# Attention of a graph network kernel: x into the output projection's banks at the start, bias rows by TensorE, softmax over heads by reduces

## The reference

```python
q = (x @ Wq + bq).reshape(N, H, HEAD)        # N = 128, H = 8, HEAD = 64
k = (x @ Wk + bk).reshape(N, H, HEAD)
v = (x @ Wv + bv).reshape(N, H, HEAD)
scores = einsum('nhd,mhd->nhm', q, k) / sqrt(HEAD)
scores = where(adj[:, None, :] == 0, -1e9, scores)
attn = softmax(scores, axis=1)               # axis 1: the heads
attn_out = einsum('nhm,mhd->nhd', attn, v).reshape(N, D_OUT) @ Wo + bo
h1 = layer_norm(x + attn_out, g1, be1)
ff = relu(h1 @ W1 + b1) @ W2 + b2
return layer_norm(h1 + ff, g2, be2)
```

## Time and profile before

| | |
|---|---|
| median of 3 runs | 244.72 us (244.4 to 245.69) |
| the profiled execution's own time | 245.73 us |
| its span | 243.8 us |
| PE busy | 230.8 us, 95% of the span |
| DVE busy | 153.4 us, 63% |
| ACT busy | 120.6 us, 49% |
| POOL busy | 6.8 us, 3% |

### The profile page before, as it was taken

How to read it: one execution, slowest core, us unless ns; L and a number is a source line. 1 busy time by engine, 2 the same in 40 slices (tenths; PEclk the granted TensorE clock), 3 DMA queues, 4 the chain that set the end, 5 groups by cost and what they waited for, 6 DMA issues and landing times.

```text
span 243.8 us, 3226 instructions
## 1 busy us (share of the span) xinstructions
PE 230.8 (95%) x1231; PEld 185.9 (76%) x1231; DVE 153.4 (63%) x271; ACT 120.6 (49%) x220; POOL 6.8 (3%) x18
## 2 busy tenths in 40 slices
PE   7999999998999999999999999999999999997980
PEld 3977788765676787888888888888888889996760
DVE  3639785577579655875856848758558454363625
ACT  0326198747729834745735646457355343244000
POOL 0020000001000000000000000000000000000001
PEclk9999999999999999999999999999999999999995
DMA  6999979930690000009022050040000000000001
GB/s 208 307 400 386 397 249 383 356 137 0 163 255 15 0 0 0 3 8 330 5 100 76 0 172 1 9 166 0 0 0 3 0 0 0 3 0 0 3 0 44
DMA packets 12320, 25.48 MB, mean 105 GB/s; under 512 B 1017, under 2 KB 1937, under 8 KB 11921
## 3 DMA queue, kind: packets, MB, share of 16 engines
q1 hardware_dynamic: 11520, 24.78, 30.0%
q10 hardware_dynamic: 784, 0.50, 0.8%
HBM read 25.01 MB, written 0.26 MB: 104 GB/s over the span
## 4 chain that ended last, share of the span: by engine, by line
PE 86%; DVE 6%; ACT 3%; issue 2%; POOL 1%; POOLq 0%; DVEq 0%; ACTq 0%
PE bank L668 36%; PE bank L651 12%; PE bank L463 9%; PE bank L472 6%; PE bank L519 4%; PE bank L535 3%; PE bank L678 3%; PE bank L679 3%; PE bank L482 2%; PE bank L446 1%; ACT WsT L408 1%; PE bank L630 1%; DVE y L884 1%; PE bank L631 1%; PE bank L635 1%
## 5 line engine op out<-in xcount | busy, mean ns | idle before, releaser
L668 PE MATMUL bank<-W2hi,Hhi 128*128 128x512 f32 x128 | 49.8, 389 | 0.0
L668 PE MATMUL bank<-W2hi,Clo 128*128 128x512 f32 x128 | 49.8, 389 | 0.0
L668 PE MATMUL bank<-W2lo,Hhi 128*128 128x512 f32 x128 | 49.8, 389 | 0.0
L380 ACT ACTIVATE Mhi<-M 128x512 fp32r<-128x512 f32 x32 | 20.2, 632 | 45.4 <-DVE M L994 45.4
L999 DVE TENSOR_TENSOR Mlo<-M,Mhi 128x512 fp32r<-128x512 f32 x32 | 22.1, 690 | 24.4 <-ACT M L381 24.4
L994 DVE TENSOR_TENSOR M<-bank,b2r 128x512 f32<-128x512 f32 x32 | 22.0, 687 | 12.6 <-PE bank L679 7.6
L668 PEld LDWEIGHTS bank<-W2hi,Clo 128*128 128x128 f32 x128 | 24.0, 188 | 5.0
L668 PEld LDWEIGHTS bank<-W2hi,Hhi 128*128 128x128 f32 x128 | 24.0, 188 | 5.0
L668 PEld LDWEIGHTS bank<-W2lo,Hhi 128*128 128x128 f32 x128 | 24.0, 188 | 5.0
L373 ACT ACTIVATE Hhi<-C 128x512 fp32r<-128x512 f32 x32 | 20.0, 625 | 12.4 <-DVE C L980 12.1
L293 ACT ACTIVATE C<-bank,cols 128x512 f32<-128x512 f32 x32 | 19.9, 685 | 11.6 <-PE bank L519 11.5
(11 more groups left out here) (193 smaller groups left out, 314.6 us busy)
## 6 DMA issues: line engine op xcount, KB each, us to landing
F<-in_L_gnn_W SPq DMA_DIRECT2D x2, 2048.0 KB, 14.3
W1raw<-in_L_gnn_W SPq DMA_DIRECT2D x1, 2048.0 KB, 22.5
ids<-in_src SPq DMA_DIRECT2D x2, 1024.0 KB, 14.0
W<-in_L_gnn_W SPq DMA_DIRECT2D x1, 2048.0 KB, 8.6
Wq<-in_L_gnn_Wq SPq DMA_DIRECT2D x4, 256.0 KB, 4.5
Wk<-in_L_gnn_Wk SPq DMA_DIRECT2D x4, 256.0 KB, 7.0
Wv<-in_L_gnn_Wv SPq DMA_DIRECT2D x1, 1024.0 KB, 10.1
ea<-in_edge_attr SPq DMA_DIRECT2D x1, 1024.0 KB, 11.8
```

What stands on the lines that cost most here:

```text
L380: act.activation(Mhi[:, t, :], M[:, t, :], ACT.Mish)
L668: done = mm(ST2[t][:, :], x[:, c, e], w[:, c, :], start=c == 0 and i == 0, stop=c == KC - 1 and i == 2)
```

## The change

- SP no longer loads bv and bo as rows of 128 partitions (256 KB each). ACT loads each into two partitions of `bvo` (two new DMA issues ahead of its others). ACT rounds them to fp32r (`bvo_parts`), and four small DVE instructions on 2 partitions make of it the high part in one partition and the rest in the other, and a `ones2` of 2 x 128. A matmul of `ones2` with `bvo_parts`, 2 rows deep, then adds the bias row: 512 columns for bv in bank 3 after v, and 256 columns for bo in each of the two banks of the projection.
- POOL's x + bo goes. x itself enters the projection's banks, which are now 5 and 6 (`O_BANKS`), at the very start, in place of the four matmuls without use.
- The scores alternate parity: for each j both parities. `scores_done` is signalled once, at the end.
- ACT's copy of parity 0 goes. DVE takes the maximum of each parity over its four heads by TENSOR_REDUCE over a view whose innermost dimension is the head (`by_heads`), and joins the two; the sum is made in the same way, parity 0 as soon as its exponential is there.
- v gets out of bank 3 by an ACT copy after the exponentials, in place of a DVE sum.
- The edge features are turned ahead of the `uniform` products, and the first group of one-hots after the attention's products. The one-hots use banks 7, 1, 2, 0 (`DT_BANKS`). F1's first two banks wait for their copies.
- ACT applies relu to F1's part i ahead of the split of W1's part i.

The diff, cut to its core (declarations of semaphores and tiles left out):

```diff
@@ sync
             sp.dma_start(Wv, w_view(a["L0_gnn_Wv"])).then_inc(S["wv_in"], 16)
-            load_row("L0_gnn_bv")
-            load_row("L0_gnn_bo")
             sp.dma_start(ea, ...)
@@ gpsimd
-            pool.wait_ge(S["x_in"], 16)
-            pool.wait_ge(row_in["L0_gnn_bo"], 16)
-            pool.tensor_tensor(xw[:, :], xs[:, :], row["L0_gnn_bo"], ALU.add).then_inc(S["xw_ready"], 1)
@@ scalar
+            for i, name in enumerate(("L0_gnn_bv", "L0_gnn_bo")):
+                act.dma_start(bvo[:, D * i:D * (i + 1)], a[name].rearrange("(o n) -> o n", o=1).to_broadcast([2, D])).then_inc(S["bvo_in"], 16)
...
+            act.wait_ge(S["bvo_in"], 32)
+            act.activation(bvo_parts, bvo, ACT.Copy).then_inc(S["bvo_hi"], 1)
             act.wait_ge(S["cols_done"], 1)
...
-                act.activation(dst[:, GE * g:GE * (g + 1)], PRE[(unit + g) % 4][:, :], ACT.Copy).then_inc(S["pre_read"], 1)
+                act.activation(dst[:, GE * g:GE * (g + 1)], DT_BANKS[g % 4][:, :], ACT.Copy).then_inc(S["pre_read"], 1)
...
-            act.wait_ge(S["scores_done"], 1)
-            act.activation(y[:, :], bank[1][:, :], ACT.Copy).then_inc(S["s_copied"], 1)
             for o in range(2):
                 act.wait_ge(S["s_centred"], o + 1)
                 act.activation(attn[:, o]...., ACT.Exp, ...).then_inc(S["exp_done"], 1)
+            act.wait_ge(S["v_done"], 1)
+            act.activation(v_sb, bank[3][:, :], ACT.Copy).then_inc(S["v_ready"], 1)
             act.wait_ge(S["ct_done"], 1)
...
             for i in range(4):
+                relu_out(i)
                 w1_high(i)
-                relu_out(i)
@@ tensor
             transpose4(bank[1], xs, S["x_transposed"])
-            keep_warm(4, bank[3])
+            start_with(O_BANKS, xs)
...
-            for o in range(2):
-                part = slice(HEAD * o, HEAD * (o + 1))
-                for j in range(KC):
-                    pe.wait_ge(S["qk_ready"], KC + j + 1)
+            for j in range(KC):
+                pe.wait_ge(S["qk_ready"], KC + j + 1)
+                for o in range(2):
+                    part = slice(HEAD * o, HEAD * (o + 1))
                     done = mm(quarter(bank[1 + o], j), kT[part, j, :], qT[part, j, :], start=True, stop=True)
-                done.then_inc(S["scores_done"], 1)
+            done.then_inc(S["scores_done"], 1)
             pe.wait_ge(S["wv_in"], 16)
-            nodes_by(bank[3], xT, Wv, S["v_done"])
+            for c in range(KC):
+                mm(bank[3][:, :], xT[:, c, :], Wv[:, c, :], start=c == 0, stop=False)
+            pe.wait_ge(S["bvo_parts"], 1)
+            mm(bank[3][:, :], ones2[:, :], bvo_parts[:, 0:D], start=False, stop=True).then_inc(S["v_done"], 1)
             pe.wait_ge(S["onehot_bf"], 2)
             count_edges(range(ET)).then_inc(S["ct_done"], 1)
-            pe.wait_ge(S["xw_ready"], 1)
-            pe.wait_ge(S["s_centred"], 2)
-            start_with((bank[1], bank[2]), xw)
+            pe.wait_ge(S["ea_in"], 16)
+            turn_features(0)
             pe.wait_ge(S["v_ready"], 1)
             pe.wait_ge(S["uniform_ready"], 1)
...
-            pe.wait_ge(S["ea_in"], 16)
-            turn_features(0)
-            pe.wait_ge(S["ident_bf_ready"], 1)
-            turn_onehots(Dbf, DT_UNIT, range(1))
...
             done.then_inc(S["ao_done"], 1)
+            pe.wait_ge(S["ident_bf_ready"], 1)
+            pe.wait_ge(S["cols_ready"], 1)
+            turn_onehots(Dbf, range(1))
+            for b in range(2):
+                mm(O_BANKS[b][:, 0:D // 2], ones2[:, :], bvo_parts[:, D + D // 2 * b:D + D // 2 * (b + 1)], start=False, stop=False)
...
             for i in range(4):
-                if i >= 2:
+                if i < 2:
+                    pe.wait_ge(S["pre_read"], 6 + i)
+                else:
                     pe.wait_ge(S["ea_lo"], 3)
@@ vector
+            sign = small[0:2, 8:9]
+            v.tensor_scalar(sign, iota_col[0:2, 0:1], -2.0, 1.0, ALU.mult, ALU.add).then_inc(S["sign_ready"], 1)
+            v.tensor_scalar(ones2[:, :], iota_row[0:2, :], 0.0, 1.0, ALU.mult, ALU.add)
+            dve.wait_ge(S["bvo_hi"], 1)
+            dve.wait_ge(S["sign_ready"], 1)
+            v.tensor_scalar(bvo_parts, bvo_parts.bitcast(F32), sign, None, ALU.mult).then_inc(S["sign_ready"], 1)
+            dve.wait_ge(S["sign_ready"], 2)
+            v.scalar_tensor_tensor(out=bvo_parts, in0=bvo, scalar=iota_col[0:2, 0:1], in1=bvo_parts.bitcast(F32), ...)
+            def by_heads(x):
+                return x.rearrange("p (j n) -> p n j", j=KC)
-            dve.wait_ge(S["scores_done"], 2)
-            dve.wait_ge(S["s_copied"], 1)
-            chain(v.tensor_tensor(y[:, :], bank[2][:, :], y[:, :], ALU.max))
-            fold(ALU.max, total[:, :])
+            dve.wait_ge(S["scores_done"], 1)
+            v.tensor_reduce(quarter(y, 0), by_heads(bank[1][:, :]), AX.X, ALU.max)
+            chain(v.tensor_reduce(quarter(y, 1), by_heads(bank[2][:, :]), AX.X, ALU.max))
+            chain(v.tensor_tensor(total[:, :], quarter(y, 0), quarter(y, 1), ALU.max))
...
-            dve.wait_ge(S["v_done"], 1)
-            v.tensor_tensor(v_sb, bank[3][:, :], r("L0_gnn_bv"), ALU.add).then_inc(S["v_ready"], 1)
-            dve.wait_ge(S["exp_done"], 2)
-            chain(v.tensor_tensor(y[:, :], attn[:, 0]...., attn[:, 1]...., ALU.add))
-            fold(ALU.add, total[:, :])
+            for o in range(2):
+                dve.wait_ge(S["exp_done"], o + 1)
+                step = v.tensor_reduce(quarter(y, o), attn[:, o].rearrange("p j n -> p n j"), AX.X, ALU.add)
+            chain(step)
+            chain(v.tensor_tensor(total[:, :], quarter(y, 0), quarter(y, 1), ALU.add))
             chain(v.reciprocal(total[:, :], total[:, :]))
```

More of the change, by code:

```diff
@@ L76, in gnn_kernel @@
         total = sb("total", [P, N])
+        ones2 = sb("ones2", [2, N], F32R)
         uniform = sb("uniform", [P, N])
@@ L147, in gnn_kernel @@
         F1_BANKS = bank[1:5]
+        DT_BANKS = (bank[7], bank[1], bank[2], bank[0])
+        O_BANKS = (bank[5], bank[6])
         TURN = (bank[3], bank[1], bank[6], bank[0])
@@ L216, in _ @@
             sp.dma_start(Wv, w_view(a["L0_gnn_Wv"])).then_inc(S["wv_in"], 16)
-            load_row("L0_gnn_bv")
-            load_row("L0_gnn_bo")
             sp.dma_start(ea, a["edge_attr_64"].rearrange("(p t) n -> p t n", p=P)).then_inc(S["ea_in"], 16)
             sp.dma_start(Wo, w_view(a["L0_gnn_Wo"])).then_inc(S["wo_in"], 16)
-            for name in EARLY_ROWS[2:4]:
+            for name in EARLY_ROWS[0:2]:
                 load_row(name)
@@ L232, in _ @@
                 sp.dma_start(other[f"ids{h}"], by_partition(a["src"][E // 2 * h:E // 2 * (h + 1)], E // 2)).then_inc(S[f"row_ids_in{h}"], 16)
-            for name in EARLY_ROWS[4:]:
+            for name in EARLY_ROWS[2:]:
                 load_row(name)
@@ L447, in transpose_halves @@
                     done.then_inc(signal, 1)
[L449 to L453, removed]
             def start_with(banks, x):
@@ L487, in free_bank, with turn_onehots @@
                 return PRE[n % 4]
-            def turn_onehots(by_edge, unit, groups):
+            def turn_onehots(by_edge, groups):
                 for g in groups:
-                    b = free_bank(unit + g)
+                    b = DT_BANKS[g % 4]
+                    if g >= 4:
+                        pe.wait_ge(S["pre_read"], g - 3)
                     for i in range(GT):
@@ L583, in _ @@
                 for b in range(2):
-                    done = columns_by((bank[1], bank[2]), aoT, Wo, b, (2 * h, 2 * h + 1), None, KC - 1)
+                    done = columns_by(O_BANKS, aoT, Wo, b, (2 * h, 2 * h + 1), None, KC - 1)
                     if h == 1:
                         done.then_inc(S["wo_done"], 1)
-            pe.wait_ge(S["cols_ready"], 1)
+            pe.wait_ge(S["s_centred"], 2)
             pe.wait_ge(S["ct_read"], 1)
-            turn_onehots(Dbf, DT_UNIT, range(1, G))
+            turn_onehots(Dbf, range(1, G))
             pe.wait_ge(S["ea_lo"], 1)
             turn_features(1)
-            transpose_halves((bank[1], bank[2]), y, S["nx_ready"], 0, S["nT_done"])
+            transpose_halves(O_BANKS, y, S["nx_ready"], 0, S["nT_done"])
             turn_features(2)
@@ L771, in _ @@
             for h in range(2):
[L772 removed]
+                pe.wait_ge(S["xw_ready"], 1 + h)
                 mm((bank[5], bank[6])[h][:, 0:D // 2], ident[:, :], half(xw, h), start=True, stop=False)
@@ L880, in _ @@
                                 ALU.is_equal).then_inc(S["onehot_bf"], 1)
-            def fold(op, dst):
-                chain(v.tensor_tensor(half(y, 0), half(y, 0), half(y, 1), op))
-                chain(v.tensor_tensor(dst, quarter(y, 0), quarter(y, 1), op))
+            sign = small[0:2, 8:9]
[5 more added lines that the diff above has]
+            dve.wait_ge(S["sign_ready"], 2)
```

(11 more changed lines are left out.)

13 lines of the change are left out of this document (7 added, 6 removed).

## The result

| | before | the change |
|---|---|---|
| median of 20 runs each | 245.14 us (244.4 to 246.08) | 244.2 us (243.69 to 244.86) |
| profiled execution | 245.73 us, span 243.8 | 244.86 us, span 243.1 |

The ratio is 0.9963, with a 95% interval of 0.9954 to 0.9973: 0.9 us, or 0.4%, less, and by the interval between 0.7 and 1.1 us. The forecast was 1.0 us less. Ratios here compare fast executions alone; one of the seven of e12 took 466.8 us and is left out of its ratio.

What follows compares the result with a forecast made beforehand. TensorE, 86% of the chain of waits, was taken as the bound, except in the softmax stretch. Only Wo's 1.0 us gain was to reach the end: 244.72 - 1.0 = 243.7 us against the median, range 242.8 to 244.8.

Steps and rivals of the forecast that it cites:

- The start: PE before q: x's four f32 passes last as long as the four unused matmuls; q starts at 6.32 as before.
- The stall: DVE's fold in the maximum, 1.45 us, waits for POOL's x + bo; removing it gives one us of DVE's 2.04.
- The scores: PE's sixteen score passes: alternating, parity 1 hides beside parity 0; all done near 15.52 instead of 16.19.
- DVE's chain: Softmax on DVE: reciprocal ends at 21.20, so the product with CTs could start 2.04 us earlier, at 21.22.
- CTs as the bound: Product with CTs: bv's row costs 0.57, CTs comes 0.05 earlier at 22.13, so 1.11 us gained, not 2.04.
- cheap-row rival: The bias row costs only its columns: CTs 0.34 earlier, no delay before Wo, gain 1.45, 243.3 us; chance 0.23.
- `uniform`: ACT's `uniform` ends 0.1 later than 21.86, near 21.96 at worst, so PE can follow before attn is ready.
- L577 and Wo: PE: L577, the first product with attn, starts at 23.23 instead of 24.34; Wo, delayed 0.1, gains 1.0 us.
- Behind Wo: Norm, one-hot copies and feed-forward run as before, 1.0 us earlier; later weights land 1.3 us earlier; relu order costs nothing.
- Given back: Rival: ACT's new order or a late landing shifts work behind Wo, PE starts no earlier: 244.7 us; chance 0.10.
- The strided rivals: DVE's reduces over strided words cost twice (244.4 us, chance 0.08) or three times (246.0 us, chance 0.05).
- The clock: Rival: with x's passes the clock rises later, q's passes cost about 2.8 us more: 246.5 us; chance 0.05.

Runs made afterwards that it cites:

- e12: Second run of the improved version (e7), on the same chip as e11; ratio to before 0.9948.
- e1: The kernel before without POOL's sum of x and bo (bo left out of the output); ratio to before 0.9999.
- e2: The change without the 2-row product of bv behind v (bv left out of the output); ratio to before 0.9954.
- e9: The change with ACT's old order, the split of W1's part i ahead of the relu of F1's part i; ratio to before 0.9962.
- e6: The change with the four matmuls without use back at the start and x's products behind the edge counts; ratio to before 0.9990.
- e7: Improved version: the change with sum by folds, DVE's edge mask before ACT's copy of CTs, first one-hots ahead of `uniform` products; ratio to before 0.9967.
- e5: The change with the scores in the old order, parity 0 whole, then parity 1; ratio to before 0.9988.
- e11: The change itself run again, unaltered, on the same chip as e12; ratio to before 0.9967.
- e3: The change with the softmax's sum made by folds as before, in place of two reduces; ratio to before 0.9975.
- e4: The change without the bv product (bv left out of the output) and with the sum by folds; ratio to before 0.9943.
- e10: The change with the maximum by folds and ACT's copy of parity 0 back, in place of reduces from PSUM; ratio to before 0.9969.
- e8: Separate kernel copying x, with DVE reduces of 512 elements at varied strides: SBUF 0.69 us at 1 and 2 words, 1.0 to 1.06 from 4; PSUM 0.69.

## Why the prediction was right

By its own steps, counted from the scores' start where the clock would blur them:

- **The start.** Forecast: x's four passes last as long as the four they replace, q starts at the same time. Shown: 1.71 and 1.71 us, q at 6.53 in both chains.
- **The stall.** Right, and e1 shows it. But I booked its 1.0 us as a gain of DVE's chain without naming what follows in the old order: PE's queue (x's products, `uniform`, features, one-hots) and DVE's own wait for v ahead of the sum. In the sum this did no harm, since the change takes x's products and the one-hots out of that queue and v's sum off DVE. Anyone who had removed the stall alone by my reading would have expected three times too much.
- **The scores.** Forecast: sixteen passes done at 15.52, 1.27 after their start. Shown: 1.26.
- **DVE's chain.** Forecast 21.20 for the reciprocal's end, 6.95 after the scores' start. Shown 22.15, 7.67: late by 0.72. Up to the end of the exponentials the walk is right to 0.01 us. The sum's reduces are the mis-sized term: 1.03 each, one behind the other, and from the exponentials' end (19.40) to the second reduce's (20.83) it is 1.43 us where I had put 0.72. I had carried the one-hots' 678 ns over to them. Those are another operation, on int32, and no run has them without a stride; the two TENSOR_SCALARs below, on 256 contiguous elements, take 411 ns each, and one on 128 (the making of `ident`, L868) takes 286, which by its slope gives some 0.66 us for 512 (an estimate). So 678 may well be their plain price, and it still said nothing of a reduce, which pays 1.03 for the stride, nor of a copy, which goes from 428 to 682. From the groups by shape of the kernel before:

```profile
L841 DVE TENSOR_SCALAR xs<-y,mv,rstd 128x256 f32<-128x256 f32 x2 | 0.7, 411 | 0.7 <-POOL rstd L271 0.7
```

- **CTs as the bound.** Forecast: the row of bv costs 0.57 (0.23 of columns, 0.34 of changing depth) and CTs comes 0.05 earlier. Shown: 0.42 in its own row and 0.12 more in the counts behind it (1.91 us, against 1.79 in e1, which has no row), 0.54; CTs 7.79 after the scores' start against 7.93 before. e2 takes the row out and gets 0.53. The cheap-row rival falls. The size is in part luck: I read 0.19 of the 0.34 from k's 32 passes taking 3.77 in place of 3.58, but F1's 32 passes, which no shallow product precedes, take 3.84 in the change's chain of waits, so those 0.19 are not shown to be a price of depth.
- **`uniform`.** I wrote that it ended at 21.86; it ended at 22.01. Nothing hung on it: in the change it ends at 22.10, and PE's `uniform` products are through before attn is ready.
- **L577 and Wo.** Forecast 1.11 and 1.0 us earlier. Shown 1.12 and, by PE's own start at 25.83, 1.03.
- **Behind Wo.** Forecast: nothing is given back. Shown: F1 1.00 earlier, the edge layer 1.0, and e9 finds no effect of ACT's new order. Given back falls.
- **The strided rivals.** "Twice" comes nearest, since the sum's reduces cost 1.5 times; the maximum's, from PSUM, cost once. DVE's 0.7 us of delay ate 0.7 of the 0.9 us of slack behind CTs, so the forecast's bound held by 0.2 us. That it held is luck: I had put all four reduces at the plain price, and had the two from PSUM cost what the two from SBUF did, DVE would have been the bound and part of the gain gone.
- **The clock.** It rises at another moment in each execution. q's 32 passes took 3.77, 3.78 and 3.57 us with the old four matmuls (before, e6, e1); with x they took 4.00 in the change and 4.13, 3.79, 3.66, 3.57 and 3.57 in e7, e12, e5, e2 and e11. The longest is 0.56 us above the shortest, not 2.8, so that rival falls. A rise as early as within the four passes was caught in four of the ten profiles with x (e3, e4, e9, e10) and in none of the three with the old matmuls, too few to tell. An estimate speaks against a difference of kind: the spans of 82 other executions of the kernel before run from 242.7 to 244.3 us, and less the 229.6 us from the scores' start to the end they put that start between 13.1 and 14.7 us, at least as early as the earliest with x (13.32).
- **The level.** The forecast of 243.7 us started from the median of three runs, 244.72; twenty runs have 245.14, and the change 244.20. So the step down was forecast well and the level was 0.5 us too low. And 0.4% can be told from no change here, which I had not granted.

The time fell by 0.9 us where this ruler has 1.0, which lies inside the interval, so nothing has to be explained. One effect should still narrow the gain in some executions: where the clock rises early, v can have to wait for Wv, which landed at 14.83, 15.12 and 15.29 in e4, e9 and e10. With the scores at 13.32 as in e9, the kernel before would have L577 at 23.41 (10.09 later) and the change has it at 22.95, a gain of 0.46 in place of 1.12. This is an estimate; no profile of the kernel before caught such an execution.

## What to carry to other kernels

When a stall goes, walk every queue that meets behind it, the matmul engine's own queue and the later waits in the stalled engine's own list too, and price each follower. The smallest slack is the gain, and an edit may be worth nothing alone and something together with another (the folds: 0 in e3, 0.18 us in e4). Compare profiles from a point behind the phase in which the clock rises, not from the start of the span. Before calling a row the plain price, find the same operation on the same size without the property in question, and do not carry it over to another operation.

## What the runs showed of the hardware

- A DVE reduce of f32 from SBUF pays one step: inner strides of 1 and 2 words 0.69 us for 512 elements, 4 words and more 1.0 to 1.06; from PSUM 0.69 at each stride (e8).
- A DVE fold of 256 columns, two inputs from SBUF, took 1.44 us beside POOL's sum of two SBUF tiles (16.87 to 18.13) and 0.42 without it (e1): it ended 0.3 us behind POOL's.
- A matmul 2 rows deep among ones 128 rows deep costs 0.54 us for its 512 columns, where a product of 512 columns at full depth takes 0.23 (four of L635 in 0.91). Passes in the two halves of the partitions run side by side: sixteen of 128 columns in 1.26 us alternating, 1.94 in blocks (e5).
- TensorE's passes stepped as at 1.2 GHz (0.43 us for 512 bf16 columns) when it began at 1.66 us, and as at 2.4 GHz from within x's products in some executions and from within q in others, with the same work ahead of it. The column of the granted clock reads 1.00 in these stretches all the same, as it did before; only the steps show the rise. The chain of waits of e3 shows an early one:

```profile
4.83 0.88 PE bank L458 x4
...
13.39 1.27 PE bank L556 x16
```

  The same four passes took 1.65 to 1.71 us in the change, e2, e5, e7, e11 and e12, and the scores start 1.1 us earlier here than in the change. The profiles' scores start anywhere from 13.3 to 14.6 us, more than the change is worth, which is likely why the times could not tell the improved version from it.
